# A transformer block and a two-way selective SSM: in every fourth state, u times B by a diagonal on PE

## The reference

```python
def _ssm(h, in_w, xproj_w, dt_bias, A_log, Dskip, out_w):
    xz = h @ in_w
    xs, z = jnp.split(xz, 2, axis=-1)
    xs = jax.nn.silu(xs)
    proj = xs @ xproj_w
    dt = jax.nn.softplus(proj[..., :D_INNER] + dt_bias)
    Bm = proj[..., D_INNER:D_INNER + D_STATE]
    Cm = proj[..., D_INNER + D_STATE:]
    A = -jnp.exp(A_log)

    def step(hst, ins):
        dt_t, B_t, C_t, x_t = ins
        dA = jnp.exp(dt_t[:, :, None] * A)
        hst = hst * dA + (dt_t * x_t)[:, :, None] * B_t[:, None, :]
        y_t = jnp.einsum('bds,bs->bd', hst, C_t)
        return (hst, y_t)
...
    y = jnp.swapaxes(ys, 0, 1) + xs * Dskip
    return y * jax.nn.silu(z) @ out_w
```

## Time and profile before

| | |
|---|---|
| median of 3 runs | 3402.99 us (3399.81 to 3408.39) |
| profiled execution | 3408.53 us |
| its span | 3406.7 us |
| PE busy | 3024.2 us, 89% |
| ACT busy | 2989.0 us, 88% |
| POOL busy | 2945.7 us, 86% |
| DVE busy | 2909.5 us, 85% |
| granted clock of PE, mean | 0.947 |

### The profile page before, as it was taken

How to read it: one execution, slowest core, us unless ns; L and a number is a source line. 1 busy time by engine, 2 the same in 40 slices (tenths; PEclk the granted TensorE clock), 3 DMA queues, 4 the chain that set the end, 5 groups by cost and what they waited for, 6 DMA issues and landing times.

```text
span 3406.7 us, 69419 instructions
## 1 busy us (share of the span) xinstructions
PE 3024.2 (89%) x21944; PEld 2683.9 (79%) x21944; DVE 2909.5 (85%) x3331; ACT 2989.0 (88%) x6469; POOL 2945.7 (86%) x1552
## 2 busy tenths in 40 slices
PE   8778898999988999899988999899998899998776
PEld 6568787888878888788877888788887888887765
DVE  3269998899888998889988999889988899899885
ACT  1189999899989999899999999899998999999994
POOL 0069998999888998889988998889988899899995
PEclk6689999999989999899999999899998999999998
DMA  4011111111111111111111111112111111111210
GB/s 174 0 42 43 48 45 47 42 51 48 43 48 47 47 47 42 49 45 48 45 47 43 49 48 43 48 41 52 48 43 46 48 47 46 42 45 45 54 47 26
DMA packets 163033, 162.50 MB, mean 48 GB/s; under 512 B 17610, under 2 KB 156874, under 8 KB 162644
## 3 DMA queue, kind: packets, MB, share of 16 engines
q1 hardware_dynamic: 162644, 157.69, 17.2%
HBM read 154.44 MB, written 3.18 MB: 46 GB/s over the span
## 4 chain that ended last, share of the span: by engine, by line
PE 45%; POOL 16%; ACT 15%; issue 13%; DVE 9%; DMA 1%; DVEq 1%; POOLq 0%; ACTq 0%; SPq 0%
POOL hst L408 12%; PE ps L1225 12%; PE ps L1241 11%; ACT dA L567 7%; PE ps L993 6%; ACT uBT L553 4%; DVE hst L892 4%; PE ps L1002 4%; POOL uBT L417 4%; PE ps L1065 3%; PE ps L1040 2%; PE ps L1114 1%; PE ps L1049 1%; PE ps L1233 1%; PE ps L1150 1%
## 5 line engine op out<-in xcount | busy, mean ns | idle before, releaser
L408 POOL TENSOR_TENSOR hst<-hst,C_sb 128x1024 f32<-128x1024 f32 x1024 | 2441.0, 2409 | 232.8 <-DVE hst L892 226.6
L892 DVE TENSOR_TENSOR_SCAN hst<-dA,ps 128x512 f32<-128x512 f32 x2048 | 2384.0, 1205 | 177.6 <-PE ps L1241 160.1
L567 ACT ACTIVATE dA<-dt,A 128x255 f32<-128x255 f32 x4096 | 1758.5, 504 | 2.8 <-DVE hst L892 2.7
L1225 PE MATMUL ps<-ident,uBT 128*128 128x128 f32 x8192 | 1288.2, 281 | 134.0 <-DVE hst L892 103.0
L1241 PE MATMUL ps<-ident,hst 128*128 128x128 f32 x8192 | 1267.9, 278 | 104.5 <-POOL hst L408 103.7
L1225 PEld LDWEIGHTS ps<-ident,uBT 128*128 128x128 f32 x8192 | 994.2, 145 | 299.0 <-DVE hst L892 152.5
L553 ACT ACTIVATE uBT<-uT,BT 128x512 f32<-128x512 f32 x1536 | 1052.2, 720 | 130.9 <-PE ps L1225 120.0
L1241 PEld LDWEIGHTS ps<-ident,hst 128*128 128x128 f32 x8192 | 979.6, 144 | 139.8 <-POOL hst L408 139.7
L417 POOL TENSOR_TENSOR uBT<-uT,BT 128x512 f32<-128x512 f32 x512 | 559.3, 1092 | 185.3 <-DVE uT L829 185.3
L476 ACT ACTIVATE probs<-ps,nmax 128x128 f32<-128x128 f32 (+1 forms) x256 | 93.9, 423 | 101.6 <-DVE nmax L764 100.7
L993 PE MATMUL ps<-xsT,w_xp 128*128 128x256 f32 x512 | 130.6, 380 | 0.0
(11 more groups left out here) (142 smaller groups left out, 2110.7 us busy)
## 6 DMA issues: line engine op xcount, KB each, us to landing
C_sb<-c_dram SPq DMA_DIRECT2D x1024, 128.0 KB, 2.9
gate_l<-gate_rows_dram SPq DMA_DIRECT2D x16, 256.0 KB, 3.7
x_att<-in_x_dram SPq DMA_DIRECT2D x8, 256.0 KB, 3.0
w<-in_L_cond_W_dram SPq DMA_DIRECT2D x2, 1024.0 KB
out_dram<-x_glu SPq DMA_DIRECT2D x8, 256.0 KB, 3.2
wg<-in_L_cond_mlp_w_dram SPq DMA_DIRECT2D x3, 512.0 KB, 11.4
w_xp<-_L_cond_fwd_xproj_w_dram SPq DMA_DIRECT2D x1, 1280.0 KB, 12.4
w_xp<-_L_cond_bwd_xproj_w_dram SPq DMA_DIRECT2D x1, 1280.0 KB, 15.0
```

What stands on the lines that cost most here:

```text
L408: pool.tensor_tensor(h, h, C_sb[:, n % FED:n % FED + 1, :].to_broadcast([P, KI, NB]), ALU.mult).then_inc(hC_ready.sem, 1)
L567: done = act.activation(dA[:, n % NT, c, lo:hi], dt[:, d, c, lo:hi], ACT.Exp, scale=A[:, d, c, n:n + 1])
L892: dve.tensor_tensor_scan(pair(hst[:, n % NR]), pair(dA[:, n % NT]), ps[:, BANK_U + (2 * n + e) % (2 * NU), :][:, way], 0.0, ALU.mult, ALU. ...
L1225: last = pe.transpose(ps[:, BANK_U + (2 * n + e) % (2 * NU), o:o + P], uBT[:, n % NF, j, c * P:(c + 1) * P], ident[:, :])
```

## The change

In every fourth state (n % 4 == 3, an odd one) the forcing is computed in another way. POOL writes two diagonal matrices of 128x128 into the first 128 columns of the two tiles of uBT: the identity times column n of BT, one for each tile of tokens. PE multiplies `uT` itself, unscaled, with that diagonal, in 8 matmuls in the places of the 8 transposes; the product has the channels on partitions and is scaled by B. ACT has nothing to make for these states, and skips them. `uBT_ready` counts 48 states per pass in place of 64.

```diff
+    by_diagonal = lambda n: n % 4 == 3
...
-        uBT_ready, uBT_pooled, uB_ready, dA_ready = flow("uBT_ready"), flow("uBT_pooled", NS // 2), flow("uB_ready", 2), flow("dA_ready", 2)
+        uBT_ready, uBT_pooled, uB_ready, dA_ready = flow("uBT_ready", NS - NS // 4), flow("uBT_pooled", NS // 2), flow("uB_ready", 2), flow("dA_ready", 2)
...
                 if r_known(p, n) >= NF:
                     pool.wait_ge(uB_ready.sem, uB_ready.at(p * NS + n, 2 - 2 * NF))
+                if by_diagonal(n):
+                    pool.tensor_tensor(uBT[:, n % NF, :, 0:P], ident[:, :].unsqueeze(1).to_broadcast([P, TT, P]),
+                                       BT[:, d, :, n:n + 1].to_broadcast([P, TT, P]), ALU.mult).then_inc(uBT_pooled.sem, 1)
+                    return
                 pool.tensor_tensor(uBT[:, n % NF, 1, :], uT[:, d, DI:2 * DI], BT[:, d, 1, n:n + 1].to_broadcast([P, DI]), ALU.mult).then_inc(uBT_pooled.sem, 1)
...
             def forcing(p, d, n):
 
+                if by_diagonal(n):
+                    return
                 r = p * NS + n
...
-            def force(p, n, e):
+            def force(p, d, n, e):
 
                 r = p * NS + n
                 if e == 0:
-                    pe.wait_ge(uBT_ready.sem, uBT_ready.at(r, 1))
+                    if not by_diagonal(n):
+                        pe.wait_ge(uBT_ready.sem, uBT_ready.at(p, n + 1 - n // 4))
                     if n % 2 == 1:
                         pe.wait_ge(uBT_pooled.sem, uBT_pooled.at(p, n // 2 + 1))
...
-                        last = pe.transpose(ps[:, BANK_U + (2 * n + e) % (2 * NU), o:o + P], uBT[:, n % NF, j, c * P:(c + 1) * P], ident[:, :])
+                        to = ps[:, BANK_U + (2 * n + e) % (2 * NU), o:o + P]
+                        if by_diagonal(n):
+                            last = pe.matmul(to, uT[:, d, j * DI + c * P:j * DI + (c + 1) * P], uBT[:, n % NF, j, 0:P], start=True, stop=True)
+                        else:
+                            last = pe.transpose(to, uBT[:, n % NF, j, c * P:(c + 1) * P], ident[:, :])
```

More of the change, by code:

```diff
@@ L1248, in state @@
                     if n + 1 < NS:
-                        force(p, n + 1, e)
+                        force(p, d, n + 1, e)
                     elif not very_last:
-                        force(p + 1, 0, e)
+                        force(p + 1, 1 - d, 0, e)
                     if n == BEHIND and e == 0:
@@ L1315, in _ @@
             for e in range(2):
-                force(0, 0, e)
+                force(0, 0, 0, e)
             period(0, False, True)
```

## The result

The change makes the kernel slower: 3454.95 us in the median of 4 runs (3454.77 to 3458.41), against 3403.38 us for the kernel before in the same session, +51.6 us, a ratio of 1.0148 (95% interval 1.0133 to 1.0163). The profiled execution took 3454.77 us.

What follows compares the result with a forecast made beforehand. A different engine was taken to bind in each stretch. Stretch terms summed to +7.75 us per block, by 7.85 blocks +61 us on 3408.5, less 5.5 for the median: 3464 us, forecast 3430 to 3500, wider range 3400 to 3535.

Steps and rivals of the forecast that it cites:

- PE's price: Each transpose swapped for an f32 matmul adds 0.1135 us: 29.1 us of PE per block, 228 us in the whole kernel.
- 1875 to 1998: Stretch with all four engines 93 to 95% busy: PE +9.6, POOL -5.3, ACT -6.5 us, counted as -2.0 us.
- Where PE is full it is paid in full: PE's added matmuls count: +2.95 us in 1802 to 1845, +3.9 in 1998 to 2070, +4.9 in 2070 to 2142.
- POOL's diagonal: A diagonal takes 0.55 us on POOL, 0.5 us less than the copy: 16 us of POOL per block.
- ACT's relief: In 1845 to 1875, where ACT is full, 2.1 copies less give -1.3 us; 20 us of ACT go per block.
- the factor 7.85: All scans, 3164 us, taken as 7.85 blocks like the one from 1802 to 2205.3 us: +7.75 us each, +61 us.
- rival 1: POOL and ACT bind where PE has room, so relief wins: -8.5 us per block, 3337 us; chance 0.10.
- The second way: Chain shares kept: L1225 +109 us, POOL's copies -31, ACT's -26, together +52 us.
- Rival 5: Added matmuls keep PE's clock at 2.4 GHz where it had fallen: -47 us, 3417 us; chance 0.06.
- Rivals 2 and 3: Matmul costs one pass like a transpose: 3314 us, chance 0.03; POOL's diagonal is dear: 3488 or 3540 us, chance 0.10.
- rival 4: PE binds nearly everywhere, so all 29.1 us per block count: +228 us, 3631 us; chance 0.08.
- More of the chain on PE: Sign expected in the changed kernel's profile: PE's share of the chain of waits grows; no size given.

Runs made afterwards that it cites:

- the relief alone: Changed kernel, but in the fourth states PE transposes unscaled u; POOL still makes the diagonal, ACT's copies are gone: 3378.68 us, ratio 0.9921 to the kernel before.
- PE's half: Kernel before, but in every fourth state PE turns the copies by an f32 matmul with the identity; ACT and POOL unrelieved: 3496.23 us, ratio 1.0267.
- twice the dose: Changed kernel with the f32 diagonal in every odd state in place of every fourth: 3596.31 us, ratio 1.0561 to the kernel before.

## Why the prediction was right

It forecast 3464 us, between 3400 and 3535, and slower; measured were 3454.95. By its steps:

- **PE's price** (0.1135 us a matmul, 29.1 us per block, from the two records of L1233) was right: 4096 records, 0.2225 us a matmul. PE's busy time grew by 166 us, not by some 200, with the granted clock higher than before. The rule of the Trainium skill (TensorE: Matmul & The Clock Gate, section Terms), a factor of four for f32, was set aside for the row; the trace of the changed kernel disagrees with it too (0.2225 us against 0.109, a factor of 2.04). The prediction's estimate of 3650 us by that rule is too low as a sum: it leaves the stretch from 1875 to 1998 at -2.0 us, though 84 swaps at 0.327 us each, an estimate from that factor, would be 27.5 us against 8.9 us free.
- **Where PE is full it is paid in full**, in these stretches: +2.8 us for +2.95 and +3.9 for +3.9. In 2070 to 2142 I counted all of 4.9 us and 3.3 were paid; some of PE's free 5.7 us did take work up. It is no rule, though: in the forward states 44 to 55 PE is as full by the profile, and nothing was paid.
- **POOL's diagonal** was estimated at 0.55 us and took 0.647 in the mean. The copies and diagonals together fell by 117.5 us (from 559.3 to 276.1 and 165.7), close to the 120 forecast; POOL's busy time as a whole fell by 95. The groups of POOL overlap in the profile (before, 2441.0 and 559.3 us in an engine that is busy for 2945.7), so the two need not agree.
- **ACT's relief** in 1845 to 1875 was the mis-sized term: -1.3 us forecast, and with the relief alone the stretch got 0.4 us shorter. ACT was busy for 29.85 of 30 us, but the chain there runs through ACT, DVE and PE in turn, and two copies less (1.3 us) shortened the stretch by 0.4. What took up the rest is not shown. With PE's addition the stretch came to +0.5, with or without the relief.
- **1875 to 1998**: -2.0 forecast, +0.8 measured; PE's share alone is +3.0, the relief's alone -2.1. The forward states 44 to 63, where the attention heads of the next block run, have POOL, DVE and ACT at 99 to 100%. They take 2.76 us a state or less before, the same with every relief, and the same with the diagonal in one state of four. POOL's 5.67 us per two states were not the bound that the sum took them for.
- **The step that failed is the factor 7.85**: the middle block's +7.75 was too low (+10.4 on the average), and the ends were taken to be like it. The last block, without a next block's layers, has POOL full and PE at 80%: rival 1 was true there, and gave 13 us back, and block 0 came out level (+1.1). Between the two traces (46 us between the spans, 52 between the medians) the middle blocks lost 62 us where 46 were forecast, and all the rest gained 16 where 14 were to be lost: two errors of opposite signs. The second way, the chain kept fixed, gave +52 us and so the measured time; but PE's share of the chain did not grow as it says, it halved. Its agreement is luck.
- **Rival 5**, the clock, was partly true: the granted clock rose from 0.947 to 0.964 in the mean. In the last stretch it rose from 0.87 to 0.94. That stretch gained 1.3 us in each of the three kernels (the change, PE's half, the relief). In PE's half nothing is relieved, so there the gain comes with PE's added work and the higher clock (0.94); with the relief alone it comes at 0.86, without the clock. What of the changed kernel's 1.3 us is the clock's stays open. Rivals 2 and 3 had no part in it. Towards rival 4 the change goes at twice the dose, where half of PE's added work is paid.
- "More of the chain on PE" was wrong as a sign to look for. Of the signs that were to prove it wrong, "POOL or ACT still full beside a shorter block" did appear, in the last block (POOL busy for 348.19 of 352.00 us).

## What to carry to other kernels

In a kernel whose four engines are all busy for 85 to 90%, price a shift of work stretch by stretch, and the first and the last round by themselves: the engine that gets the work can pay in full where it is full, and the one relieved gives back only where it alone is. Count the records of an existing instruction of the same form before pricing a new one; here two records for an f32 product against one for a transpose decided the result. Then put the work only where the timing by state, with the change in it, shows that it is free; a busy share does not show it. The same idea that cost 1.5% in every fourth state gained 1.3% in chosen ones.

## What the runs showed of the hardware

- An f32 matmul of 128x128 by 128 columns is two records of 0.111 us each at full clock (0.89 us for eight), in float32r it is one record, and a transpose of f32 data is one of 0.109 us.
- The first four states of a forward pass are shorter where PE's granted clock is higher: in block 5 they take 13.9 us at 0.75 (before), 11.8 at 0.86 (the changed kernel) and 11.5 at 1.00 (PE's change alone). The two with the shorter times have 0.9 us more work for PE in these states.
- Less work on POOL lengthened a stretch in which PE's clock then fell: with POOL relieved, alone or with ACT, the clock went to its lower level, 1.2 GHz, at the same state of all six middle blocks (2.4 us more for four states), and with ACT alone relieved it did not. In the kernel with both, 1.8 us of more work on PE per block removed this and made the backward pass 2.0 us shorter. PE's busy time just before the fall was the same with and without it.
- A chain of waits can move from one engine to another (PE's share from 45 to 22%) although the work was added on the first and costs time there. Where several engines are level, its shares did not tell which one to relieve.
- POOL's product of 128x256 with two broadcast operands takes 0.62 to 0.65 us, the 128x512 one 1.08 us.
